# Graph layer on one core: dst columns read from the converted table, and a new split of the late row gathers

## What is computed

```
h    = relu(layernorm(x))
w    = silu(silu(edge_attr_8 @ W1 + b1) @ W2 + b2) @ W3 + b3      # 256 weights per edge
m    = messages(h[src], edge_attr_4, w)                           # 32 values per edge
out  = x + self(h; Ws, Wv) + segment_sum(m, dst) / 4
```

## Time and profile before

| | |
|---|---|
| median of 3 runs | 605.76 us (603.63 to 607.81) |
| profiled execution, its own time | 603.84 us |
| span of its trace | 601.7 us |
| mean granted TensorE clock | 0.812 |
| busy, share of the span | PE 87%, weight load 68%, DVE 69%, ScalarE 68%, POOL 80% |

### The profile page before, as it was taken

How to read it: one execution, slowest core, us unless ns; L and a number is a source line. 1 busy time by engine, 2 the same in 40 slices (tenths; PEclk the granted TensorE clock), 3 DMA queues, 4 the chain that set the end, 5 groups by cost and what they waited for, 6 DMA issues and landing times.

```text
span 601.7 us, 14157 instructions
## 1 busy us (share of the span) xinstructions
PE 521.4 (87%) x3255; PEld 411.0 (68%) x3255; DVE 413.3 (69%) x1147; ACT 408.9 (68%) x1219; POOL 482.5 (80%) x387
## 2 busy tenths in 40 slices
PE   5879897989988799698999999999899999899530
PEld 4768786868875576576777777777777777677530
DVE  5766977966784687567667777777767877778140
ACT  3425464546356977678778897898979978989510
POOL 6777777777777777888888888888888888888887
PEclk9859899989697858578677897788878888887555
DMA  4646665556441001222222222222222222222222
GB/s 130 196 114 188 168 181 186 171 159 197 137 137 28 15 14 13 11 11 10 12 10 11 12 11 10 11 11 10 12 11 11 12 10 11 11 10 12 11 9 9
DMA packets 54019, 34.51 MB, mean 57 GB/s; under 512 B 37638, under 2 KB 41400, under 8 KB 53944
## 3 DMA queue, kind: packets, MB, share of 16 engines
q0 software_dynamic: 34048, 6.22, 19.2%
q1 hardware_dynamic: 11958, 14.65, 8.3%
q10 hardware_dynamic: 7938, 12.86, 5.9%
HBM read 17.59 MB, written 16.08 MB: 56 GB/s over the span
## 4 chain that ended last, share of the span: by engine, by line
POOL 73%; issue 24%; DMA 3%; POOLq 0%
POOL out_dram L334 44%; POOL xg L321 29%; DMA out_dram<-sums,idx_i 2%; DMA src_all<-in_src_dram 0%; POOLq L352 0%; POOLq L340 0%; POOLq L353 0%; POOLq L347 0%
## 5 line engine op out<-in xcount | busy, mean ns | idle before, releaser
L334 POOL DMA_INDIRECT out_dram<-sums,idx_i x196 | 305.6, 1559 | 59.8 <-issue 58.6
L321 POOL DMA_INDIRECT xg<-in_x_dram,src_all x182 | 176.0, 967 | 56.5 <-issue 55.2
L735 PE MATMUL ps<-msg,eq 128*128 128x32 f32 (+1 forms) x980 | 131.3, 284 | 15.8 <-DVE msg L1074 15.3
L735 PEld LDWEIGHTS ps<-msg,eq 128*128 128x128 f32 x980 | 127.7, 206 | 16.0 <-DVE msg L1074 15.5
L1040 DVE TENSOR_TENSOR prod<-ps,coef 128x256 f32<-128x256 f32 (+1 forms) x245 | 98.7, 470 | 17.2 <-PE ps L684 15.4
L502 ACT ACTIVATE dsq<-ps,dcol 128x512 f32<-128x512 f32 x196 | 87.8, 549 | 0.2 <-PE ps L697 0.2
L527 ACT ACTIVATE eq<-dsq,onecol 128x384 f32<-128x384 f32 x147 | 73.8, 525 | 4.1 <-issue 4.1
L684 PE MATMUL ps<-w3blk,x 64*128 64x256 f32 x392 | 75.8, 519 | 0.0
L684 PEld LDWEIGHTS ps<-w3blk,x 64*128 64x128 f32 x392 | 45.6, 253 | 37.8 <-issue 32.5
L386 ACT ACTIVATE sqT<-ps 128x512 f32<-128x512 f32 (+2 forms) x50 | 29.3, 585 | 61.7 <-PE ps L623 61.4
L1003 DVE SCALAR_TENSOR_TENSOR first<-sums,rank_max,dmt_all 128x4 f32<-128x4 f32 x49 | 10.9, 223 | 87.5 <-ACT sums L488 87.5
(11 more groups left out here) (106 smaller groups left out, 842.4 us busy)
## 6 DMA issues: line engine op xcount, KB each, us to landing
xg<-in_x_dram SPq DMA_DIRECT2D x1320, 0.1 KB
xin<-in_x_dram SPq DMA_DIRECT2D x48, 256.0 KB, 3.0
out_dram<-oc ACTq DMA_DIRECT2D x48, 256.0 KB, 2.7
xg<-in_x_dram ACTq DMA_DIRECT2D x384, 0.1 KB
out_dram<-sums,idx_i POOLq DMA_INDIRECT x196, 3.1
xg<-in_x_dram,src_all POOLq DMA_INDIRECT x182, 2.9
er_all<-in_edge_attr_dram SPq DMA_DIRECT2D x1, 780.0 KB
sh_all<-in_edge_attr_dram SPq DMA_DIRECT2D x1, 390.0 KB
```

The lines of the kernel that those rows point to most:

```text
L321: pool.indirect_dma_start(xg[:, t * D:(t + 1) * D], None, x, bass.IndirectOffsetOnAxis(ap=src_all[:, t:t + 1], axis=0)).then_inc(signal, 16)
L334: pool.indirect_dma_start(out, bass.IndirectOffsetOnAxis(ap=idx_i[:, k % NS, a:a + 1], axis=0), sums[:, k % NS, a * DR:a * DR + D], None, ...
L735: m = pe.matmul(psSUM[:, a * DR:a * DR + n], eq[:, k % 2, o:o + P], msg[:, k % 2, b, 0:n], start=(b == a), stop=(not carried and (b == a - ...
```

## The change

POOL gathers 180 tiles instead of 182; RT is 16 and RA 5. ScalarE's queue fetches tiles 180 to 183 and 192 (640 rows), SP's queue 184 to 191 and 193 to 195 (1320 rows, as before). ScalarE's rows stand at five places of a batch, three at each. The late units are then 30, 30, 12 and 4 tiles. `dcol` and its copies go: PE's transposes and ScalarE's squares read `dst_f` itself, and the two engines wait once for its conversion instead of once per batch for the copy.

```diff
--- before.py
+++ after.py
@@ -64,14 +64,16 @@
 
 
 
-    GT, RT, RA = 10, 14, 3
+
+    GT, RT, RA = 10, 16, 5
     G1 = T + 1 - RT
-    G2 = G1 + RA
     EW = UT * NB
     GF = EARLY * GT
     PASSES = NU // 2
     LATE_UNITS = [range(GF, GF + 30), range(GF + 30, G1), range(G1, NU * UT), range(NU * UT, T + 1)]
     LATE = len(LATE_UNITS)
+    ACT_TILES = [*range(G1, G1 + RA - 1), NU * UT]
+    SP_TILES = [t for t in range(G1, T + 1) if t not in ACT_TILES]
     GW = max(len(tiles) for tiles in LATE_UNITS)
 
     CENTRED = {0: EARLY, 1: EARLY + 1, PASSES - 3: EARLY + 2}
@@ -158,7 +160,6 @@
         outer = sb("outer", [P, BT, 3 * MUL])
         msg = sb("msg", [P, 2, BT, DR])
 
-        dcol = sb("dcol", [P, NS, BT])
         dsq = sb("dsq", [P, BT * BW])
         eq = sb("eq", [P, 2, BT * BW])
         lcnt = sb("lcnt", [P, NS, BT])
@@ -199,7 +200,7 @@
             gsum_done gc_done gsq_done gvar_done gstd_done grstd_done h_done
             erT_ready erT_copied l1_ready x1_done l2_ready x2_done
             dot_done coef_done tp_ready prod_done red_done outer_done msg_done
-            dcol_done dT_ready sq_done eq_done first_done idxf_done idx_done
+            dT_ready sq_done eq_done first_done idxf_done idx_done
             sum_ready sums_done scattered scattered_next scattered_last idxc_done carry_done er_loaded rows_at dve_zero b3_scaled""".split()
         s = {n: sem(n) for n in names}
         x_loaded = [sem(f"x_loaded{i}") for i in range(XS)]
@@ -279,7 +280,7 @@
 
             sp.dma_start(out[N:N + BT * P, :].rearrange("(p r) d -> p (r d)", p=P), spare0[:, :]).then_inc(s["spare_stored"], 16)
 
-            late_rows = iter([(t, p) for t in range(G2, T + 1) for p in range(P if t < T else TAIL)])
+            late_rows = iter([(t, p) for t in SP_TILES for p in range(P if t < T else TAIL)])
             OF_ROWS = (RT - 1) * P + TAIL
             offsets = []
 
@@ -425,13 +426,7 @@
                     act.wait_ge(s["tp_ready"], 2 * u - 2)
                 act.activation(x2[:, k % 2, 0:w], psMLP[:, 0:w], ACT.Silu, bias=b2col[:, :]).then_inc(s["x2_done"], 1)
 
-            def dst_col(q, k):
-
-                if k >= NS:
-                    act.wait_ge(s["sq_done"], q - NS + 2)
-                act.activation(dcol[:, k % NS, :], dst_f[:, ds(q * BT, BT)], ACT.Copy).then_inc(s["dcol_done"], 1)
-
-            rows_of_tiles = iter([(t, p) for t in range(G1, G2) for p in range(P)])
+            rows_of_tiles = iter([(t, p) for t in ACT_TILES for p in range(P)])
             offsets = []
 
             def gather_rows(count):
@@ -464,10 +459,6 @@
                     feat_std(n - 1, GT)
                 if base % 4 == 3 and base >= 7:
                     feat_square(n, GT)
-                if base == FULL:
-                    act.wait_ge(s["dst_cast"], 1)
-                    for q in range(3):
-                        dst_col(q, q)
 
             for k in range(DBODY):
                 node_step(k, k, 0)
@@ -490,17 +481,17 @@
             def dst_square(q, k):
 
                 act.wait_ge(s["dT_ready"], q + 1)
-                act.wait_ge(s["dcol_done"], q + 1)
                 if k >= 1:
                     act.wait_ge(s["eq_done"], q)
                 if k >= 1:
 
-                    act.activation(csq[:, 0:2 * P], psDT[:, 2 * P:BW], ACT.Square, bias=dcol[:, (k - 1) % NS, 0:1], scale=-1.0)
-                    act.activation(csq[:, 2 * P:3 * P], psDT[:, 3 * P:BW], ACT.Square, bias=dcol[:, (k - 1) % NS, 1:2],
+                    act.activation(csq[:, 0:2 * P], psDT[:, 2 * P:BW], ACT.Square, bias=dst_f[:, (q - 1) * BT:(q - 1) * BT + 1],
                                    scale=-1.0)
+                    act.activation(csq[:, 2 * P:3 * P], psDT[:, 3 * P:BW], ACT.Square,
+                                   bias=dst_f[:, (q - 1) * BT + 1:(q - 1) * BT + 2], scale=-1.0)
                 for b in range(BT):
                     m = act.activation(dsq[:, b * BW:b * BW + (BT - b) * P], psDT[:, b * P:BW], ACT.Square,
-                                       bias=dcol[:, k % NS, b:b + 1], scale=-1.0)
+                                       bias=dst_f[:, q * BT + b:q * BT + b + 1], scale=-1.0)
                 m.then_inc(s["sq_done"], 1)
 
             def dst_equal(q, k):
@@ -531,6 +522,7 @@
             act.wait_ge(s["w_loaded"], 16 * (2 + 8 + UT))
             for c in range(NCH - 2, NCH):
                 store(c, c)
+            act.wait_ge(s["dst_cast"], 1)
             act.wait_ge(s["rows_at"], 1)
             mlp_in(0, 0)
             mlp_one(0, 0)
@@ -561,9 +553,9 @@
                         feat_std(roots, width(roots))
                     if not end:
                         mlp_one(u + 2, k + 2, 2 * P if last else 4 * P)
-                        dst_col(q + 3, kq + 3)
+                    gather_rows(3)
                     dst_equal(q + 1, kq + 1)
-                    gather_rows(2)
+                    gather_rows(3)
                     if h == 1 and squares is not None:
                         feat_square(squares, width(squares))
                     gather_rows(3)
@@ -572,9 +564,9 @@
                     gather_rows(3)
                     if not end:
                         mlp_two(u + 2, k + 2, 2 * P if last else 4 * P)
-                        dst_col(q + 4, kq + 4)
+                    gather_rows(3)
                     dst_equal(q + 2, kq + 2)
-                    gather_rows(2)
+                    gather_rows(3)
 
             for v in range(3):
                 edge_pass(v, v == 0, False, SCALED.get(v), CENTRED.get(v))
@@ -688,13 +680,13 @@
 
             def dst_rows(q, k):
 
-                pe.wait_ge(s["dcol_done"], q + 1)
                 if k >= 1:
                     pe.wait_ge(s["sq_done"], q)
                 else:
+                    pe.wait_ge(s["dst_cast"], 1)
                     pe.wait_ge(s["o_done"], NCH - 1)
                 for b in range(BT):
-                    m = pe.transpose(psDT[:, b * P:(b + 1) * P], dcol[:, k % NS, b:b + 1].to_broadcast([P, P]), ident[:, :])
+                    m = pe.transpose(psDT[:, b * P:(b + 1) * P], dst_f[:, q * BT + b:q * BT + b + 1].to_broadcast([P, P]), ident[:, :])
                 m.then_inc(s["dT_ready"], 1)
 
             def node_step(c, base):
```

## The result

| | before | after |
|---|---|---|
| median | 605.62 us (603.32 to 607.81, 6 runs) | 618.16 us (615.65 to 623.50, 6 runs) |
| ratio, 95% interval | | 1.0212 (1.0179 to 1.0245) |
| profiled execution, its span | 603.84, 601.7 us | 615.65, 613.9 us |
| granted clock, mean | 0.812 | 0.808 |

The forecast of 603.3 us failed; what came is the outcome of rival B. A second session gave 620.92 us and 1.022 (1.013 to 1.031).

A forecast was written before the change was run, and what follows sets the result against it. POOL was taken as the bound, its scatters and gathers filling 97% of the span. Its -2.51 us for two gathers, with 0 for the rest, took the median from 605.76 to 603.3 us, range 601.0 to 607.5.

The forecast's parts named there:

- rival B: ScalarE becomes the bound, deciding at 0.41 us more per batch: 612.5 or 631.1 us; chance 0.11.
- What bounds before: POOL bounds the kernel from end to end, its scatters and gathers with issue gaps making 97% of the span.
- (1) The gathers: Two gathers fewer on POOL, 1.256 us each: first scatter and end come 2.51 us sooner.
- (2) Rows: Four more rows a batch in ScalarE's queue stay hidden: 0 us per row, bounds 0 to 0.32 us.
- (2) Loads: Eight more address loads in ScalarE's queue, 1.0 us exposed each: 8 us over 43 batches, bounds 0 and 19.
- (2) Absorption: ScalarE waits 40 us for TensorE's sums between 180 and 560 us; load losses come partly off that.
- (3) Columns: 49 column copies dropped from ScalarE, 0.10 us each: 4.9 us saved, off POOL's path.
- (4) Late unit: The late unit of 12 tiles finds its SP and ScalarE rows fetched with 12 us to spare: cost 0.
- (5) SP's end: SP's queue ends 2.2 us later, 8 ns per added ScalarE row, bounds 0 and 4.9; 2.66 us are left.
- rival A: SP finishes later and the last batch takes the end: 605.5 us at 4.9 us later; chance 0.21.

The follow-up runs named there:

- e10: Changed kernel with POOL at 181 tiles, ScalarE's queue at 512 rows, 13 a batch, loads of 16 addresses behind the squares: 604.19 us, ratio 0.9961.
- e4: Changed kernel with ScalarE's queue loading addresses once instead of 20 times, 608 of 640 rows reusing the first 32 addresses: 603.58 us, ratio 0.9965.
- c1: Changed kernel run again, unaltered, in another session: 620.92 us, ratio 1.022 to the kernel before.
- e5: Changed kernel with 16 addresses per load, once a batch behind the squares: 820.93 us, ratio 1.0004, with long node phase; again, 610.33 us, 0.9985.
- e6: Kernel before with one load of 32 addresses per unit, always inside the equality step: 827.95 us, ratio 1.0057, with long node phase; again, 606.19 us, 1.002.
- e2: Kernel before with the columns part alone, targets read from the converted table and the old split kept: 606.43 us, ratio 1.0003.
- e3: Kernel before with the new split alone, POOL 180 tiles and ScalarE's queue 15 rows a batch, copied columns kept: 625.35 us, ratio 1.028.
- e1: Changed kernel with 30 addresses loaded once per unit, behind the squares of the unit's first batch: 660.03 us, ratio 1.086.

## Why the prediction was wrong, point by point

**What bounds before: right.** e10 gains 0.4% once the rest of the machine keeps ahead of POOL; e4's 0.35% points the same way, its interval just reaching 1.

**(1) The gathers: right, though the profiled execution hides it.** The page has 180 gathers, 176.3 us busy at a mean of 979 ns; the 182 of before had 176.0 us at 967. The first scatter of after started at 234.34, so 0.22 us early and not 2.51. But the same kernel again (c1) had it at 232.63. Over the nine profiled executions with 180 gathers and the short node phase it is 232.6 on the mean (231.1 to 234.3), over the three with 182 it is 234.8 (234.4 to 235.4): 2.2 us apart. The term holds, give or take a microsecond or two in a single execution.

**(2) Rows: right.** The bound 0 taken for one more row is what e4 shows at 15 rows a batch, with 1.5 us of "issue" idle in all. The rule of the Trainium skill that the prediction cites (Perfetto Trace Analysis, the section on DVE and Act engine instructions) agrees with it. At 20 rows a batch the kernel is 0.5% slower than before.

**(2) Loads: the step that failed.** The prediction took 1.0 us for an exposed load, 8 us for eight more, and "issue" idle near 20 us. The count of 20 was right; the trace of after has 32.7 us for them, so 1.6 us each, on the old loads as well as the new. Rows and loads were costed one by one, each against the same spare time: the 2.8 us left over in a batch without a load were given to the four rows, and the load in the next batch was given them again. By these numbers 11 rows a batch leave the queue 4.3 us busy of 7.4 (3.5 of rows, 0.8 of loads), 15 rows 5.9 us (4.8 and 1.1). Then, a unit has 30 rows and a load comes every 32, so nearly each unit has a load, and at nearly the same place as in the unit before; in the kernel before the place moved by ten rows. The runs show that both matter. With the same short loads at the same places the idle time per load is 0.14 us at 13 rows a batch (e10: 4.6 us for 32) and 0.6 at 15 (e5: 24.9 for 40). With the rows of before and a load that always falls inside the equality step it is 1.4 us instead of 1.0 (e6: 25.9 for 19). How the two share after's 1.6 us is not shown.

**(2) Absorption: wrong.** "What it loses on a load comes partly off" the 40 us of waits for TensorE, said the prediction. From the indices of batch 12 to those of batch 43 these waits grew, in after and before:

```profile
ACT sums L479 <- PE ps L730: 26.2, 12, 3.1
```

```profile
ACT sums L488 <- PE ps L738: 20.1, 12, 3.2
```

Instead of taking something off the 15.3 us they added 6.1. ScalarE and TensorE wait for each other by turns: in the unit above a late copy of ScalarE makes TensorE idle, and its next products run at the lower clock, so ScalarE waits again for the sums. Over 310 to 545 us the granted clock is 0.81 for 0.85 before, and the products of L676 take 548 ns on the mean in 330 to 480 us, 482 before. A wait in such a loop is no spare time. The clock also falls where TensorE has no gap (0.64 in 250 to 275 us before, with TensorE busy throughout), and how the loss divides between idle time and clock stays open.

**(3) Columns: right where POOL is the bound** (e2: no difference). Where ScalarE is, e3 is 4.4 us slower than c1 and 7.2 slower than after, around the 4.9 us of the working, but from different sessions and within the intervals.

**(4) Late unit: right**; no wait for its rows.

**(5) SP's end: the 8 ns a row were noise.** SP's last row went out at 571.6 in after, 570.9 before, and at 573.1 in e2, which has ScalarE's rows of before. The range over all runs with the short node phase, 571 to 574 us, does not go with ScalarE's rows. Of what the Trainium skill (Perfetto Trace Analysis, the section on HWDGE DMA instructions) says of the shared descriptor generator, these totals show no effect; only single rows were longer, 0.71 us at most in SP's queue in after. Where POOL was the bound with 15 rows a batch, the last batch kept 3.3 us of slack (e4), more than the 2.66 of the working, so rival A did not come. Batch 48 is late in after (POOL waits at 604.8) since its predecessors are, not by SP.

**Rival B: right in outcome and sign, its price in part by luck.** POOL waits for VectorE's indices from batch 26 on, as B said it would. It was to decide at 0.41 us more per batch; 0.73 came. By its formula, with the slack of 9.5 us: 31 x (8.04 - 7.44) - 9.5 = 9.1 us late by batch 43, and its two prices, 612.5 and 631, enclose 618. But it priced four exposed rows (1.28 us a batch) with next to nothing for the loads (0.03), and e4 shows the reverse: the rows were hidden, the loads were not. What was also wrong is its chance, 0.11. The evidence against it was one batch with 11 rows and no load in it.

## What to carry to other kernels

A queue's spare time can be spent once. Before giving a queue more to issue, add up all that it does in the period (DMAs, register loads, hand-overs), on the fullest period and not on a quiet one, and treat waits between two engines that feed each other as no reserve. Then step by less: 13 rows with short aligned loads beneath running work gained 0.4%, 15 rows with long loads where they fell lost 2%. And see that a second queue does not set the end of an experiment, as SP's did where the node phase was long. And watch the slack beside the time: e6 loses all of its slack and no time.

## What the runs showed of the hardware beyond the expected

A register load's time goes with the number of addresses (0.83 us for 8, 1.20 for 16, 2.24 for 32 in ScalarE's queue), and a load of 30 that begins 8 bytes past a multiple of 16 takes 6.6 us instead of 2.3 (e1). The same kernel can need 821 us in one session and 606 in another, on the same chip. Most of that lies ahead of POOL's first scatter: the kernel of e5 took 814.2 us of span against 605.2, and 185 of these 209 us had passed when its first scatter began (417.0 against 231.7).
